# Four graph layers on one core: a finer last unit, another form of the state update, norms on ScalarE, row sums and bias additions on VectorE, and a start that streams one batch

## The chip, the cores and the metric

The kernel runs on one core of a Trainium2 chip. The time is the device time of one execution in microseconds (us). Its engines are TensorE (PE: matmuls, with PEld for their weight loads), VectorE (DVE), ScalarE (ACT), GpSimd (POOL) and SyncE (SP, whose queue starts most DMAs). On-chip memory is SBUF; matmuls write to the eight banks of PSUM, 128 rows of 512 fp32 each.

## The reference, cut to what matters

B = 8 batches of x with N = 1024 nodes and D = 128 features, and one adj of 1024 x 1024. Four layers follow each other, each as x = layernorm(x + layer(x)):

```python
# layer 0
adj @ (x @ W0) + b0
# layer 1
res = si[:, :, None] + sj[:, None, :] + adj * w_r + g_b    # si, sj = x @ w_i, x @ w_j
(res @ x) @ W1 + b1
# layer 2
x_h = elu(x @ Wi + bi)
e = sigmoid(a_tgt[:, :, None] + a_src[:, None, :] + be) * mask   # from x_h; mask from adj
recv = concat(e @ x_h, x_h * e.sum(-1))
concat(elu(recv @ Wn + bn), x_h) @ Wm + bm
# layer 3, five steps, in_matrix = out_matrix = adj
av = concat(adj @ h, adj @ h); u3 = h @ u3_w.T + u3_b
z = sigmoid(av @ w3_w.T + w3_b + u3)
r = sigmoid(av @ w4_w.T + w4_b + u3)
hv = tanh(av @ w5_w.T + w5_b + (r * h) @ u5_w.T + u5_b)
h = (1.0 - z) * h + z * hv
```

## The kernel before

**Precision.** Products with adj and those of layer 3 split each factor in a high part (rounded to fp32r by a ScalarE copy) and a low part (what is left, a DVE subtraction called `lo`, L1023), and add hi x hi, hi x lo and lo x hi: three matmuls in place of one. `adj_product` (L617 to L624) does it for one half of 512 columns: 8 tiles x 3 = 24 matmuls of 128x512. The other matmuls take plain fp32.

**Pieces and units.** Layers 0 to 2 of a batch are cut into named pieces: `x0` (load and split), `m0a m0b` (product with adj, by halves), `y0a y0b` (weights and sum with x), `v0` (statistics of the norm), `n0` (its power -0.5 and application), then `l1`, `d1` (split, row dots), `sums`, `rows`, `m1`, `y1`, `v1`, `n1` of layer 1, and `t2`, `pj`, `th`, `tg`, `as`, `s00` to `s17`, `e00` to `e17`, `rs`, `rv`, `y2`, `v2`, `n2` of layer 2. `s01` is a sigmoid of one tile (ScalarE, L907) and its product with the mask (DVE, L1168) in a ring of three slots; `e01` the matmul on it (L719); its row sums are added tile by tile by GpSimd (L591), and `rsa` (L725) broadcasts them. GpSimd also adds the bias rows b0 and bm to x (`add_bias`, L562) and takes each norm's power (L574, L602, L605).

Layer 3 runs in 40 units, one for a step of a batch; two batches alternate. Unit u makes `state_product` for its own batch and, between the pieces of that, the candidate and the update of the unit before. Its DVE update (L1195 to L1203) is

```python
v = v - hT        # L1198, after tanh
v = v * z         # L1200
hT = hT + v       # L1202
```

A table written by hand or by a planner (`TABLES`) gives for each engine the order of the pieces: a `first` list that runs before unit 0, and for each unit the numbered gaps (`@4`) in which pieces are put. Each engine follows its own list in order; semaphores join them. Batches 0 to 3 are mostly prepared ahead of unit 0 and in units 0 to 7; batches 4, 5 from unit 10, and 6, 7 from unit 20 on. After a batch's fifth step the next unit takes its statistics (`output_stats`) and, at its end, applies the norm on DVE (`output_apply`, L1046); SP stores it.

**Start.** SP loads x of batch 0, one tile of adj, x of batch 1, the other seven tiles, then weights and x of batches 2 and 3. ScalarE and DVE split each tile as it comes; TensorE multiplies batches 0 and 1 with each tile (L829 to L840), 12 matmuls a tile, after both batches have been split.

**End.** After unit 39 (batch 7, step 5) the candidate, the update, the turn back, the sum with x, eight statistics, the power, eight applications and one store of 512 KB follow one another.

## Time and profile before

| | us |
|---|---|
| median of 3 runs | 1278.41 (1275.87 to 1279.11) |
| the profiled execution | 1275.51 |
| its span in the trace | 1273.7 |
| TensorE busy | 1221.2 |
| VectorE busy | 924.8 |
| ScalarE busy | 587.7 |
| GpSimd busy | 267.5 |
| mean granted TensorE clock | 0.987 |

The span runs from the first instruction to the last one in the trace; the execution's own time is 1.8 us more. A busy time counts each moment once in which the engine worked on something. A granted clock of 1.00 is 2.4 GHz, 0.50 is 1.2 GHz.

### The profile page before, as it was taken

How to read it: one execution, taken by the hardware profiler on the slowest of the kernel's cores; microseconds unless marked ns; L12 is line 12 of the kernel's file. 1: busy time of each engine (PE TensorE's matmuls, PEld its weight loads, DVE VectorE, ACT ScalarE, POOL GpSimd, SP SyncE). 2: the span in 40 equal slices, each digit the busy share in tenths (PEclk: the TensorE clock that was granted, in tenths of full speed). 3: DMA queues.
4: the chain of work that ended last, by engine and by line, in shares of the span. 5: the costliest groups of instructions: out<-in, count | busy, mean ns of one | idle time of the engine just before them, and what ended most of it. 6: DMA issues, size and time to landing. Idle time of an engine off the chain costs nothing.

```text
span 1273.7 us, 15433 instructions
## 1 busy us (share of the span) xinstructions
PE 1221.2 (96%) x5488; PEld 937.0 (74%) x5488; DVE 924.8 (73%) x2154; ACT 587.7 (46%) x857; POOL 267.5 (21%) x174
## 2 busy tenths in 40 slices
PE   6988889999999999999999999999999999999994
PEld 5866457577777888877787688886787688888883
DVE  6999776867766586679587676688777768655656
ACT  4225653546654434355345553336446544444451
POOL 3115561511420010035013311024202500000001
PEclk9989999999999999999999999999999999999997
DMA  7212221200200011012002101102101200000001
GB/s 242 100 58 82 78 90 42 83 26 1 91 18 1 1 34 59 1 40 86 9 1 67 42 1 38 54 1 76 58 1 33 75 2 17 17 1 1 1 1 33
DMA packets 38459, 52.70 MB, mean 41 GB/s; under 512 B 2736, under 2 KB 19632, under 8 KB 38384
## 3 DMA queue, kind: packets, MB, share of 16 engines
q1 hardware_dynamic: 38240, 51.33, 12.2%
q8 instruction: 44, 0.72, 0.2%
q0 software_dynamic: 144, 0.40, 0.1%
q14 instruction: 31, 0.25, 0.1%
HBM read 43.32 MB, written 8.39 MB: 41 GB/s over the span
## 4 chain that ended last, share of the span: by engine, by line
PE 85%; DVE 9%; issue 2%; ACT 2%; POOL 1%; DMA 1%; POOLq 0%; SPq 0%; DVEq 0%; ACTq 0%
PE ps L622 44%; PE ps L719 7%; PE ps L627 6%; PE ps L629 6%; PE ps L628 6%; PE ps L633 4%; PE ps L640 3%; PE ps L837 2%; PE ps L732 1%; PE ps L725 1%; PE ps L733 1%; DVE x L1046 1%; DVE ring L1168 1%; PE ps L700 1%; PE ps L681 1%
## 5 line engine op out<-in xcount | busy, mean ns | idle before, releaser
L622 PE MATMUL ps<-adj_hi,xh 128*128 128x512 f32 x656 | 282.2, 430 | 3.6 <-DVE xl L1023 2.5
L622 PE MATMUL ps<-adj_hi,xl 128*128 128x512 f32 x656 | 257.2, 392 | 0.0
L622 PE MATMUL ps<-adj_lo,xh 128*128 128x512 f32 x656 | 256.4, 391 | 0.0
L622 PEld LDWEIGHTS ps<-adj_hi,xh 128*128 128x128 f32 x656 | 123.7, 189 | 41.8 <-issue 15.5
L622 PEld LDWEIGHTS ps<-adj_lo,xh 128*128 128x128 f32 x656 | 123.9, 189 | 32.4 <-issue 10.6
L591 POOL TENSOR_TENSOR fr<-fr,ring 128x512 f32<-128x512 f32 x84 | 125.0, 1488 | 106.0 <-DVE ring L1168 102.9
L622 PEld LDWEIGHTS ps<-adj_hi,xl 128*128 128x128 f32 x656 | 123.3, 188 | 27.1
L1168 DVE TENSOR_TENSOR ring<-ring,mk 128x512 f32<-128x512 f32 x128 | 102.3, 832 | 39.5 <-ACT ring L907 39.3
L1186 DVE TENSOR_TENSOR r<-r,hT 128x512 f32<-128x512 f32 x80 | 71.2, 907 | 77.8 <-ACT r L960 77.8
L863 ACT ACTIVATE mh<-ps 128x512 fp32r<-128x512 f32 x80 | 47.7, 596 | 167.3 <-PE ps L622 167.3
L719 PE MATMUL ps<-ring,fz 128*128 128x512 f32 x224 | 109.6, 600 | 4.2 <-DVE ring L1168 3.9
L1023 DVE TENSOR_TENSOR ml<-ps,mh 128x512 fp32r<-128x512 f32 x80 | 55.1, 688 | 76.9 <-ACT mh L863 76.6
L627 PE MATMUL ps<-mh,wh 128*128 128x512 f32 x240 | 104.5, 435 | 1.6 <-DVE ml L1023 1.5
L907 ACT ACTIVATE ring<-fh,asrcm 128x512 f32<-128x512 f32 x112 | 77.1, 718 | 48.2 <-PE ps L719 30.1
L629 PE MATMUL ps<-ml,wh 128*128 128x512 f32 x240 | 93.9, 391 | 0.0
L628 PE MATMUL ps<-mh,wl 128*128 128x512 f32 x240 | 93.7, 390 | 0.0
L863 ACT ACTIVATE xh<-ps 128x512 fp32r<-128x512 f32 x64 | 38.1, 595 | 117.3 <-PE ps L633 117.3
L627 PE MATMUL ps<-th,wh 128*128 128x512 f32 x160 | 73.7, 461 | 2.5 <-DVE tl L1023 2.5
L960 ACT ACTIVATE r<-ps,cols 128x512 f32<-128x512 f32 x80 | 54.5, 689 | 46.1 <-PE ps L629 45.6
L602 POOL TENSOR_TENSOR rso<-veo,mhalf 128x8 f32<-128x8 f32 x7 | 12.6, 1802 | 292.2 <-DVE veo L1041 292.2
L952 ACT ACTIVATE z<-ps,cols 128x512 f32<-128x512 f32 x80 | 54.1, 687 | 36.9 <-PE ps L629 36.6
L719 PEld LDWEIGHTS ps<-ring,fz 128*128 128x128 f32 x224 | 40.9, 191 | 35.2 <-issue 21.0
...
## 6 DMA issues: line engine op xcount, KB each, us to landing
mk<-mask_scratch SPq DMA_DIRECT2D x128, 256.0 KB, 2.9
...
```

Source lines behind the costliest of these rows:

```text
L591: tell(pool.tensor_tensor(f["r"][:, cut(h)], before, ring[:, k % RING, :], ALU.add), "rs_" + name[1:], b)
L622: mm = pe.matmul(dst, a[:, t, :], b[:, t, cut(h)], start=(t == 0 and i == 0), stop=(t == T - 1 and i == 2))
L627: pe.matmul(dst, wh[:, k, :], hi, start=first, stop=False, skip_group_check=True)
L628: pe.matmul(dst, wl[:, k, :], hi, start=False, stop=False, skip_group_check=True)
L629: return pe.matmul(dst, wh[:, k, :], lo, start=False, stop=last, skip_group_check=True)
L719: tell(pe.matmul(ps[:, BANKS_B[b][h], :], f["z"][:, tile(t)], ring[:, place[b, h, t] % RING, :], start=(t == 0), stop=(t == T - 1)), "ag" ...
L863: return act.activation(dst, src, ACT.Copy)
L907: tell(act.activation(ring[:, k % RING, :], f["h"][:, cut(h)], ACT.Sigmoid, bias=f["asrc"][:, t:t + 1]), "sg" + name[1:], b)
L960: act.activation(r[:, cut(h)], ps[:, GB + h, :], ACT.Sigmoid, bias=rb).then_inc(r_done, 1)
L1023: return dve.tensor_tensor(dst, src, hi.bitcast(F32), ALU.subtract)
L1168: tell(dve.tensor_tensor(ring[:, k % RING, :], ring[:, k % RING, :], mk[:, k % RING, :], ALU.mult), "ma" + name[1:], b)
L1186: dve.tensor_tensor(r[:, cut(h)], r[:, cut(h)], hT[s][:, cut(h)], ALU.mult).then_inc(rh_done, 1)
```

## The change

1. **Last unit by halves.** Unit 39 gets an order of its own (`ending`) on TensorE, ScalarE and DVE: gates, reset and candidate of half 0 (512 columns) run inside and behind the product of half 1, and the last batch's output is normed and stored as two halves. The second half's norm is applied on DVE.
2. **Update** as v = v z; hT = v - (z - 1) hT. The product (z - 1) hT (`keep`) is made before tanh, after the low part of the reset.
3. **Norms applied on ScalarE**, as Identity(scale x + bias) with scale rs and bias nb = -mean rs, a new 128x8 product on GpSimd behind the power. The mean's factor is -0.5 in place of 0.5.
4. **Row sums and bias additions on DVE**: each tile's addition stands right behind its mask product; new pieces `c0` and `c2` add the bias rows.
5. **Batch 0 alone streams**: batch 1's x is loaded after all of adj, and its m0 runs as ordinary pieces.
6. All four tables have a new order.

The orders, cut to the first lists of TensorE, ScalarE and DVE and a few units:

```diff
     "PE": """
-first m0a:0 m0b:0 m0a:1 m0b:1 y0a:0 y0b:0 y0a:1 y0b:1 m0a:2 m0b:2 y0a:2 y0b:2 m1a:0 m1b:0 sums:0 m1a:1
-first rows:0 y1a:0 m1b:1 y1b:0 sums:1 rows:1 y1a:1 t2a:0 t2b:0 pja:0 pjb:0 y1b:1 tha:0 thb:0 tga:0 tgb:0
-first m1a:2 m1b:2 e00:0 e01:0 e02:0 sums:2 e03:0 e04:0 e05:0 t2a:1 t2b:1 rows:2 y1a:2 e06:0 e07:0 pja:1
...
-first pja:2 pjb:2 e10:1
+first m0a:0 m0b:0 y0a:0 y0b:0 m0a:1 m0b:1 y0a:1 y0b:1 m0a:2 m0b:2 m1a:0 m1b:0 sums:0 m1a:1 rows:0 y1a:0
+first m1b:1 y1b:0 sums:1 y0a:2 y0b:2 rows:1 y1a:1 y1b:1 t2a:0 t2b:0 pja:0 pjb:0 tha:0 thb:0 tga:0 tgb:0
+first m1a:2 t2a:1 m1b:2 e00:0 e01:0 e02:0 e03:0 t2b:1 e04:0 sums:2 pja:1 e05:0 e06:0 e07:0 rows:2 rsa:0
+first pjb:1 y1a:2 y1b:2 e10:0 rva:0 e11:0 tha:1 e12:0 e13:0 thb:1 y2a:0 tga:1 tgb:1 e14:0 e15:0 e16:0 e17:0
+first rsb:0 rvb:0 e00:1 e01:1 e02:1 m0a:3 y2b:0 e03:1 e04:1 e05:1 m0b:3 e06:1 e07:1 y0a:3 y0b:3 t2a:2 t2b:2
+first e10:1
...
     "ACT": """
+first x0:0 x0:1 x0:2 m0a:0 m0b:0 weights:0 m0a:1 m0b:1 n0:0 m0a:2 n0:1 m0b:2 m1a:0 m1b:0 m1a:1 m1b:1 n1:0
+first t2a:0 t2b:0 pja:0 pjb:0 n0:2 tha:0 thb:0 tga:0 tgb:0 n1:1 s00:0 s01:0 s02:0 t2a:1 m1a:2 m1b:2 s03:0
...
     "DVE": """
-first x0:0 x0:1 x0:2 weights:0 mask:0 mask:1 mask:2 y0a:0 mask:3 y0b:0 y0a:1 v0:0 y0b:1 mask:4 n0:0 v0:1
-first l1:0 d1:0 n0:1 mask:5 l1:1 d1:1 sums:0 mask:6 y0a:2 mask:7 rows:0 y0b:2 y1a:0 v0:2 y1b:0 v1:0 sums:1
-first n0:2 n1:0 rows:1 pja:0 pjb:0 y1a:1 y1b:1 l1:2 as:0 v1:1 s00:0 s01:0 s02:0 d1:2 n1:1 s03:0 s04:0 s05:0
+first x0:0 c0:0 x0:1 x0:2 y0a:0 c0:1 weights:0 y0b:0 mask:0 v0:0 mask:1 c0:2 y0a:1 y0b:1 mask:2 v0:1 l1:0
+first d1:0 mask:3 l1:1 d1:1 mask:4 mask:5 mask:6 sums:0 mask:7 rows:0 y1a:0 y1b:0 v1:0 sums:1 y0a:2 y0b:2
+first rows:1 v0:2 c2:0 y1a:1 pja:0 pjb:0 y1b:1 v1:1 l1:2 as:0 d1:2 s00:0 s01:0 s02:0 s03:0 s04:0 s05:0 s06:0
+first c2:1 s07:0 sums:2 pja:1 rows:2 s10:0 rsa:0 s11:0 pjb:1 s12:0 s13:0 y1a:2 rva:0 y1b:2 v1:2 s14:0 s15:0
...
     "POOL": """
+first n0:0 n0:1 n1:0 n0:2 n1:1 n1:2 n2:0 n0:3 n1:3 n2:1 n2:2 n2:3
```

The code, cut to its core (the first `ending` is that of TensorE, the second that of DVE; `norm_apply` is ScalarE's):

```diff
             load(0)
             for t in range(T):
                 sp.dma_start(stage[t], adjT[tile(t), :]).then_inc(s_adj[t], 16)
-                if t == 0:
-                    load(1)
+            load(1)
...
+            def ending(now, prev):
+                s, p, i = now
+                state_product(s, 0, p, i, prev, {})
+                for h in range(2):
+                    candidate(*prev, halves=(h,))
+                for h in range(2):
+                    from_state(s, h, p, i, prev)
+                state_product(s, 1, p, i, prev, {1: lambda: (update_gate(s, 0, p, i), turn_state(prev[0], 0, *prev[1:])),
+                                                 2: lambda: turn_state(prev[0], 1, *prev[1:]),
+                                                 4: lambda: reset_gate(s, 0, p, i),
+                                                 6: lambda: candidate_start(s, 0, p, i, prev)})
+                candidate(*now, halves=(0,))
+                update_gate(s, 1, p, i)
+                candidate_start(s, 1, p, i, prev)
+                reset_gate(s, 1, p, i)
+                turn_state(s, 0, p, i)
+                candidate(*now, halves=(1,))
+                turn_state(s, 1, p, i)
...
+            def norm_apply(src, small_, tiles):
+                _, _, _, rs, nb = small_
+                for t in tiles:
+                    ins = act.activation(src[:, t, :], src[:, t, :], ACT.Identity, bias=nb[:, t:t + 1],
+                                         scale=rs[:, t:t + 1])
+                return ins
...
-            def update(s, p, i, fill=lambda: None):
-                for h in range(2):
+            def keep(s, p, i, halves=(0, 1)):
+                for h in halves:
+                    dve.wait_ge(rh_done, nth(p, i, s, h))
+                    dve.scalar_tensor_tensor(out=hT[s][:, cut(h)], in0=z[:, cut(h)], scalar=1.0, in1=hT[s][:, cut(h)],
+                                             op0=ALU.subtract, op1=ALU.mult).then_inc(kept, 1)
+
+            def update(s, p, i, fill=lambda: None, halves=(0, 1)):
+                for h in halves:
                     dve.wait_ge(v_done, nth(p, i, s, h))
-                    dve.tensor_tensor(v[:, cut(h)], v[:, cut(h)], hT[s][:, cut(h)], ALU.subtract).then_inc(d_sub, 1)
-                    dve.wait_ge(d_sub, nth(p, i, s, h))
                     dve.tensor_tensor(v[:, cut(h)], v[:, cut(h)], z[:, cut(h)], ALU.mult).then_inc(d_mul, 1)
+                    dve.wait_ge(kept, nth(p, i, s, h))
                     dve.wait_ge(d_mul, nth(p, i, s, h))
-                    dve.tensor_tensor(hT[s][:, cut(h)], hT[s][:, cut(h)], v[:, cut(h)], ALU.add).then_inc(h_new, 1)
+                    dve.tensor_tensor(hT[s][:, cut(h)], v[:, cut(h)], hT[s][:, cut(h)], ALU.subtract).then_inc(h_new, 1)
                     fill()
...
+            def ending(now, prev):
+                s, p, i = now
+                m_split(s, 0, p, i)
+                update(*prev)
+                state_lo(prev[0], 0, *prev[1:])
+                state_lo(prev[0], 1, *prev[1:])
+                reset(s, p, i, halves=(0,))
+                output_stats(B - 2)
+                reset_lo(s, p, i, halves=(0,))
+                keep(s, p, i, halves=(0,))
+                output_moments(B - 2)
+                m_split(s, 1, p, i)
+                update(*now, halves=(0,))
+                reset(s, p, i, halves=(1,))
+                state_lo(s, 0, p, i)
+                reset_lo(s, p, i, halves=(1,))
+                keep(s, p, i, halves=(1,))
+                output_stats(B - 1)
+                update(*now, halves=(1,))
+                output_moments(B - 1)
+                state_lo(s, 1, p, i)
+                output_stats(B)
+                output_moments(B)
+                output_apply(B)
```

## Rows read from the trace of the kernel before

**Rows 1.** The page, section 1: busy us (share of the span) xinstructions.
```profile
PE 1221.2 (96%) x5488; PEld 937.0 (74%) x5488; DVE 924.8 (73%) x2154; ACT 587.7 (46%) x857; POOL 267.5 (21%) x174
```

**Rows 2.** Busy time by stretch: length, each engine, granted clock, DMA share, GB/s.
```profile
0.00:96.00 96.00, 79.84 (x385) 65.79 (x386) 81.61 (x241) 27.08 (x33) 21.89 (x22) 0.95 0.38 133
96.00:178.00 82.00, 70.35 (x281) 44.08 (x280) 66.42 (x191) 45.57 (x61) 43.56 (x27) 0.98 0.25 81
178.00:240.00 62.00, 58.49 (x247) 40.22 (x246) 51.31 (x169) 26.50 (x37) 22.80 (x14) 0.95 0.16 51
240.00:1234.00 994.00, 990.55 (x4482) 769.72 (x4481) 697.84 (x1483) 477.96 (x711) 175.98 (x110) 1.00 0.09 29
1234.00:1274.00 40.00, 21.97 (x100) 17.17 (x98) 27.59 (x73) 10.61 (x17) 3.27 (x2) 0.83 0.09 26
```

**Rows 3.** Groups by form: 1100 to 1230 us, 96 to 240 (two), whole run (two).
```profile
L1186 DVE TENSOR_TENSOR r<-r,hT 128x512 f32<-128x512 f32 x14 | 9.6, 692 | 24.3 <-ACT r L960 24.3
...
L1168 DVE TENSOR_TENSOR ring<-ring,mk 128x512 f32<-128x512 f32 x39 | 29.6, 796 | 1.8 <-ACT ring L907 1.8
...
L1168 DVE TENSOR_TENSOR ring<-ring,mk x39: 672/682/2068, 100.0 to 239.4; 128x512 f32<-128x512 f32 x39
...
L1186 DVE TENSOR_TENSOR r<-r,hT 128x512 f32<-128x512 f32 x80 | 71.2, 907 | 77.8 <-ACT r L960 77.8
...
L591 POOL TENSOR_TENSOR fr<-fr,ring 128x512 f32<-128x512 f32 x84 | 125.0, 1488 | 106.0 <-DVE ring L1168 102.9
```

**Rows 4.** Timeline of the start (start, length, engine); first row: the chain.
```profile
11.11 23.80 PE ps L837 x96
...
7.54 1.23 DVE L1023 TENSOR_TENSOR adj_lo<-fh,adj_hi 128x1024 fp32r<-128x1024 f32 x1
...
11.11 0.77 PE L837 MATMUL ps<-adj_hi,fxh 128*128 128x512 f32 x1 [11.11 <-DVE xl L1023]
...
14.25 3.42 DVE L1023 TENSOR_TENSOR adj_lo<-fk,adj_hi 128x1024 fp32r<-128x1024 f32 x1
...
18.68 1.07 ACT L863 ACTIVATE adj_hi<-v 128x1024 fp32r<-128x1024 f32 x1 [0.28 <-DMA v<-in_adjT]
...
24.87 2.62 DVE L1060 TENSOR_TENSOR mk<-mk 128x128 f32<-128x128 f32 x3 [0.40 <-DMA mk<-in_u]
```

**Rows 5.** Timeline around m1a of batch 2, rsa of batch 0, and unit 0.
```profile
94.50 1.21 DVE L1023 TENSOR_TENSOR tl<-x,th 128x1024 fp32r<-128x1024 f32 x1
...
95.77 0.50 PE L622 MATMUL ps<-adj_hi,th 128*128 128x512 f32 x1
...
119.89 2.25 POOL L591 TENSOR_TENSOR fr<-fr,ring 128x512 f32<-128x512 f32 x1
...
122.19 1.13 PE L725 MATMUL ps<-fr,ones 128*128 128x512 f32 x2 [1.38 <-POOL fr L591]
...
177.65 0.50 PE L622 MATMUL ps<-adj_hi,xh 128*128 128x512 f32 x1 [2.16 <-DVE xl L1023]
```

**Rows 6.** Groups of ScalarE by form, whole run.
```profile
L952 ACT ACTIVATE z<-ps,cols 128x512 f32<-128x512 f32 x80 | 54.1, 687 | 36.9 <-PE ps L629 36.6
...
L863 ACT ACTIVATE mh<-ps 128x512 fp32r<-128x512 f32 x80 | 47.7, 596 | 167.3 <-PE ps L622 167.3
L863 ACT ACTIVATE th<-r 128x512 fp32r<-128x512 f32 x80 | 47.2, 624 | 2.9 <-DVE r L1186 2.5
L863 ACT ACTIVATE th<-hT 128x1024 fp32r<-128x1024 f32 x40 | 42.1, 1051 | 0.0
...
L863 ACT ACT_TABLE_LOAD x1 | 1.3, 1283 | 0.7 <-PEq L1311 0.7
```

**Rows 7.** Timeline of the tail.
```profile
1259.69 0.63 PE L633 MATMUL ps<-ident,hT 128*128 128x128 f32 x4 [3.22 <-DVE hT L1202]
...
1263.59 1.64 DVE L1028 BATCH_NORM_STATS2 sto<-x 128x6 f32<-128x128 f32 x8
...
1267.84 2.14 DVE L1046 TENSOR_SCALAR x<-x,mvo,rso 128x128 f32<-128x128 f32 x8 [1.75 <-POOL rso L605]
```

More of the change, by code:

```diff
@@ L46 @@
+unit3 @2 t2b:3 @10 pja:3 @12 pjb:3 @16 tha:3 @17 thb:3 tga:3 @22 tgb:3
+unit4 @1 e00:3 @9 e01:3 @11 e02:3 @15 e03:3 @16 e04:3 e05:3 @17 e06:3 @18 e07:3 @20 rsa:3 @21 e10:3 @22 e11:3 @23 e12:3 @24 e13:3 rva:3 e14:3 @27 e15:3
+unit5 @11 e16:3 e17:3 y2a:3 @14 rsb:3 @16 rvb:3 @22 y2b:3
+unit6
+unit7
 unit8
 unit9
[L48 to L51 removed]
```

490 lines of the change are left out of this document (255 added, 235 removed).

## Prediction

> **What bounds the kernel now.** I read the page first: its engine line [rows 1] shows TensorE busy for 1221.2 of 1273.7 us, VectorE (DVE) for 924.8. Then the table by stretch [rows 2], with its granted clock. From 240 to 1234 us TensorE is busy for 990.55 of 994 us at full clock: nothing that shortens another engine's work can show there. TensorE's idle time is 16.16 us before 96 us, 11.65 us from 96 to 178, 3.51 us from 178 to 240 and 18.03 us after 1234: 49.4 us in all, and in those stretches the clock is 0.95, 0.98, 0.95 and 0.83, so some matmuls run at 1.2 instead of 2.4 GHz. The change does not alter what TensorE computes, so it can win only there: in the head (to 240) and in the tail.
>
> In the head DVE is busy for 81.61 of 96 us and 66.42 of 82. The views by line and form say with what, and that GpSimd (POOL) makes it slower: r times h takes 692 ns where GpSimd is silent and 907 ns over the whole run; the mask product 796 ns from 96 to 240 although its median is 682 and its longest 2068 [rows 3]. So the question is what the new division of work does to DVE, and to the chains through it, before 240 us.
>
> **The start.** The first matmul is at 11.11 us [rows 4]. It waits for the low part of batch 1, though the first tile of adj is split at 7.54 + 1.23 = 8.77. With batch 0 alone it starts at about 8.8: 2.3 us won. Batch 0 brings 6 matmuls a tile; 96 matmuls take 23.80 us in the chain, the first nine of them at about 0.43 us and the rest at 0.227. Six at full speed take 1.4 us, and tiles arrive about every 1.3 us. GpSimd's first two bias additions, beside which one split took 3.42 instead of 1.23 us, are gone, and batch 1's 512 KB leave the queue between the tiles. The last tile, copied at 18.68 now, should be copied by 17.4 to 18.5 and split by 19.8; TensorE ends the stream at 21.2. Then y0 of batch 0 waits for ScalarE (the x copies of batches 1 and 2, then mc0a): 1.3 us idle. m0 of batch 2 starts at 36.9, against 38.48 now. The gain shrinks from 2.3 to 1.5 us.
>
> A first common mark is m1a of batch 2, because both orders have the same TensorE pieces ahead of it; it starts at 95.77 now, behind the low part of that batch, which DVE ends at 94.50 + 1.21 = 95.7 [rows 5]. Against that list DVE's new one has, ahead of the same point, four bias additions more (a 1024-column operation each, 1.22), the statistics v1 of batch 1 (1.64 + 0.9 = 2.55), four norm applications less (2.1 each), and it loses what GpSimd costs three sums of weights (2.62 us for three, where 128 columns take some 0.3 each: 1.8) [rows 4]: 4.9 + 2.5 - 8.4 - 1.8 = -2.8, which gives 92.9; ScalarE's norm ahead of the split, 1 us longer, makes it 93.9. TensorE's idle time there stays much as it is (5.05 us between 60 and 96; my layout of the new order has 4.3 ahead of the turn of x_h, 2.3 ahead of m1a:2, 1.7 in smaller pieces), and a us of slow clock goes with it: 94.8, so **-1 us**.
>
> **96 us to unit 0, now at 177.65** [rows 5]. TensorE takes 81.9 us for 66.8 us of work (pja and pjb of batch 2, 0.86 each, move behind unit 0's start: 65.1 afterwards). What was added to DVE: 31 row-sum additions at 0.69 (21.4 us) and three bias additions at 1.22 (3.7). What was taken off: six norm applications, which together take 17.6 us there. What GpSimd's contention costs there, from the forms against their quiet values (39 mask products at +0.114 are 4.4 us [rows 3]; the norm instructions, row dots, bias sums and clamps of that stretch make up the rest): about 18 us, of which 5 sit in the norm applications and 3 stay with GpSimd's remaining powers at 1.7. So 25.1 - 17.6 - 10 = -2.5 us: DVE's load is about the same, a little less.
>
> What changes more is the chains. Row sums took 1.49 us each on GpSimd [rows 3], and bias additions stand between them: the last one of batch 0's first half runs from 119.89 to 122.14, and the matmul on it waits till 122.19 [rows 5], though its mask product was done at 116.5. On DVE the addition stands 0.7 us behind the mask product. ScalarE also waits for GpSimd's sums to free the three ring slots. Against that, ScalarE's m1b copy now stands ahead of s03, which leaves DVE idle for some 4.5 us after s02. Laying both lists out on those durations, TensorE idles for 7.2 us (0.4 ahead of rows:2, 1.4 of e10:0, 1.1 of y2a:0, 0.4 of e14, 1.5 of rsb:0, 2.2 of rvb:0, 0.2 of m0a:3) and unit 0 starts at 166.2 + 1.7 (for the moved pieces) = 167.9, 9.7 us ahead. I take 1 us off this for the start's share (counted above), 2 for two ScalarE norms on the chain at +1 us each (below) and 2 for small waits and a half-speed stretch or two: **-5 us**, bounds 0 and -9.
>
> **Norms on ScalarE.** No row shows an application with two per-partition operands. DVE's eight instructions take 2.14 us in all [rows 7]. On ScalarE a copy of 128x512 from SBUF takes 624 ns and 128x1024 1051, so 0.83 ns a column and 0.2 us fixed; a per-partition bias makes 596 into 687, so +0.09 [rows 6]. With bias and scale: 0.107 + 0.2 + 0.18 = 0.48 us, less about 0.1 of overlap (the ring activations): 0.38, eight of them 3.1 us. Bounds 2.0 (plain copies of 128 columns) and 3.9. GpSimd adds a 128x8 product, 0.2 to 0.3 us. So each norm's chain grows by 1.0 + 0.3. Outside the head TensorE hides it: ScalarE is busy for 478 of 994 us, and the next split of m is 2.8 us away. All copies together cost one table load [rows 6]; I assume that Identity needs none either.
>
> The Trainium skill's page "ScalarE: Activation LUTs", section "Rules for kernel authors", speaks against this part: additions and products belong on VectorE. The rows bear it out for one instruction. That is rival 2.
>
> **Update as z v - (z - 1) h.** Three DVE instructions a half remain; one moves ahead of tanh. From tanh to the new state it is 2 x 0.72 instead of 3 x 0.72. In the full units TensorE never waits for it: 0. A scalar_tensor_tensor takes 750 ns where a product takes 690, 80 x 0.06 = 5 us of DVE, hidden by the 30% that DVE is idle there. Without that cover it would cost at most those 5.
>
> **The full units**: 0, bounds -2 (3.45 us are idle) and +4 (a 3.1 us output norm against a ScalarE gap of 2.8 in seven units, if the surplus always shows with its restart).
>
> **The tail** [rows 7]. Now: TensorE waits 3.22 us for the update alone; the statistics stand at 1263.59, power 1.64, application 2.14 to 1269.98, then a store of 3.7. Afterwards, with the same last-unit start of 1233.79: both products and their inserts end at 1250.1 (all passes at 0.68, turns 0.4). In the half order, r h of half 0 is at 1248.4, but batch 6's statistics (1.64) come ahead of its split, and its moments (0.9) ahead of m_split of half 1, so ml is ready only at 1253.0. Then reset gate 1255.4, r and its split 1258.5, tanh 1260.05, product and difference 1261.55, turn, moments of half 0, sum with x 1263.2, statistics and moments of four tiles 1.75, power 1.64, application of four tiles 1.07: 1267.7. **-2.3 us**, bounds 0 and -4.
>
> **Sum**: 1275.5 (that execution's time; span 1273.7 and 1.8 around it) - 1 - 5 + 0 - 2.3 = 1267.2. The median of the runs is 2.9 above that execution: 1270.1, so **1270**.
>
> **Rivals.**
> 1. The gain is the walk's in full: -1.5 - 9.7 - 2.3 and 1.5 more from a shorter unit 0: 15 us, 1263. For it: DVE's contention vanishes. Against: the walk has no small waits. The Trainium skill, "SBUF — State Buffer", section "Who interferes with whom", has a VectorE instruction with two SBUF inputs blocked whole while GpSimd reads; [rows 3] agree (2068 against 682 ns).
> 2. ScalarE's applications lengthen the chains: nine norms lie in the head, each +1.3 us. If all are on TensorE's path that is 11.7 us, of which I counted 2; the head's 6 us are gone and only the tail stays: 1276. For it: the idle gaps now sit at norms (81.3 to 85.5 us). Against: DVE does other work meanwhile.
> 3. Slower: DVE becomes longer. Per batch +14 x 0.69 + 2 x 1.22 - 3 x 2.1 = +5.8 us; four batches in the head make 23 us. It decides where contention gives back under 4 us a batch and the DVE list, not a chain, sets the pace: +10 of those 23 in view less the tail's 2 gives 1286. Against: the measured contention, 18 us for under three batches.
> 4. The new order works, but the tail alone shows, since ScalarE blocks on m1b and the ring waits come back: -2 to -3, 1276.
>
> **Chances.** Forecast 1270: 0.52; rival 1: 0.20; rivals 2 and 4 together: 0.18; rival 3: 0.10. A measurement of this kernel tells about 0.3% (3.8 us) from nothing. Faster: the forecast, rival 1 and a little of 2: 0.77; same 0.15; slower 0.08. The range leaves out rival 3 and half of rival 1's far side: 1259 to 1277; the forecast's own is 1266 to 1274.
>
> **What would show it.** Right: first matmul near 8.8; unit 0's first matmul (the first wait for the low part of batch 0's state) near 171; mask products near 690 ns; ScalarE applications near 0.38 us apart; still one table load for copies; the full units at over 99.5%; the last application ending some 2 us nearer to unit 39's start. Wrong: DVE over 90% busy from 96 to 178, TensorE waiting for norms, or idle time in the full units.

## The result, and the profile after

The changed kernel takes 1264.18 us (median of 4 runs, 1263.86 to 1265.89) against 1277.28 for the kernel before beside it; the ratio is 0.9902, 95% interval 0.9885 to 0.9918. It is faster by 13 us; 1270 was forecast. The profiled execution took 1264.36 us, its span is 1262.6, so 1.8 us lie around the span as before. Ratios are taken over executions of the fast state; one execution of a later kernel (e11) took 2549.81 us, in the slow state, and is not in its ratio.

The engine line of the page, which answers to [rows 1]:

```profile
PE 1217.9 (96%) x5488; PEld 935.6 (74%) x5488; DVE 870.5 (69%) x2037; ACT 683.0 (54%) x1109; POOL 73.2 (6%) x79
```

TensorE's work is the same 5488 matmuls; VectorE lost 54 us, GpSimd 194, ScalarE gained 95. The table by stretch, with the columns of [rows 2] and bounds moved to the new marks:

```profile
0.00:96.00 96.00, 77.45 (x383) 63.57 (x384) 76.53 (x242) 39.00 (x65) 14.89 (x24) 0.98 0.38 133
96.00:170.00 74.00, 68.17 (x275) 42.73 (x274) 57.57 (x159) 51.08 (x81) 5.41 (x4) 0.99 0.27 86
170.00:240.00 70.00, 65.72 (x271) 44.86 (x272) 54.56 (x165) 40.13 (x69) 6.61 (x6) 0.95 0.19 61
240.00:1222.00 982.00, 979.59 (x4446) 763.85 (x4445) 656.25 (x1404) 535.24 (x865) 42.16 (x40) 1.00 0.09 29
1222.00:1263.00 41.00, 26.92 (x119) 20.63 (x117) 25.59 (x70) 17.55 (x32) 4.12 (x5) 0.86 0.09 26
```

Before 96 us TensorE idles for 18.55 us, 2.4 more than before; from 96 us to unit 0 it idles for 5.8 us, where [rows 2] give 11.65. The middle is 99.8% busy.

TensorE's busy time fell too, by 3.3 us for the same 5488 matmuls, because less of it lies at the lower of the two clock levels (granted clock 0.50): before unit 39, the kernel before is there from 79.8 to 90.0, 124.1 to 127.5, 178.8 to 182.2 and 236.8 to 240.2 us, the changed kernel from 91.2 to 98.1 and 231.2 to 238.1. In these stretches it is busy for 17.2 against 10.7 us, and half the difference is 3.3 us. So of the 11.1 us between the two spans 7.8 are idle time of TensorE (52.5 and 44.7 us), and the other 3.3 are what the clock is worth.

The timeline of TensorE: the first matmul, y0 of batch 0, and unit 0's first matmul, against [rows 4, 5]:

```profile
8.68 0.77 PE L855 MATMUL ps<-adj_hi,fxh 128*128 128x512 f32 x1 [8.68 <-DVE adj_lo L1078]
...
22.81 2.02 PE L631 MATMUL ps<-wf,fm 128*128 128x128 f32 x16 [1.06 <-ACT fm L878]
...
170.43 0.80 PE L613 MATMUL ps<-adj_hi,xh 128*128 128x512 f32 x1
```

The first matmul is 2.4 us earlier and unit 0 7.2 us earlier. Between them lies the mark, m1a of batch 2. This is the chain of work (start, length, what) that leads to it:

```profile
83.33 1.57 DVE stAp L1086 x8
...
85.83 2.59 POOL rsAp L572
...
88.49 0.21 POOL nbAp L574
...
88.73 3.19 ACT x L883 x8
91.95 1.06 ACT th L878
93.00 0.49 ACT fz L878
93.50 0.14 issue
93.63 3.75 PE ps L702 x4
97.39 2.65 PE ps L613 x10
```

TensorE pipelines its matmuls, so the first one of the mark is drawn from 96.40 on, beside the end of those before it; the second is the safer mark. The first row is the low part of batch 2, which the mark needs:

```profile
93.04 1.23 DVE L1078 TENSOR_TENSOR tl<-x,th 128x1024 fp32r<-128x1024 f32 x1
...
97.61 0.61 PE L613 MATMUL ps<-adj_lo,th 128*128 128x512 f32 x1
```

In the kernel before it starts at 96.11, 0.34 us behind the row in [rows 5], so the mark is now **1.5 us later**. TensorE waits 3.10 us at 93.63 for `fz`, ScalarE's copy of `tha` of batch 0. ScalarE could not make it, for the norm of batch 2 (its eight applications and the rounding) stands ahead of it in its list. That wait is not the mark waiting for batch 2: its low part is done at 94.27, 3.3 us ahead. It is another batch's copy queued behind a norm. The norm in its turn starts when VectorE's statistics and GpSimd's power of 2.59 us are done; VectorE works without a break from 74.54 to 85.77 on this chain.

The four matmuls that waited then take 3.75 us, at a granted clock of 0.50, where the kernel before has, at 1.00:

```profile
94.00 2.04 PE L711 MATMUL ps<-fk,we2b 128*128 128x512 f32 x4
```

The groups by form, whole run, which answer to [rows 3] (VectorE) and [rows 6] (ScalarE):

```profile
L1227 DVE TENSOR_TENSOR ring<-ring,mk 128x512 f32<-128x512 f32 x128 | 87.2, 686 | 35.1 <-ACT ring L933 35.1
L1234 DVE TENSOR_TENSOR fr<-fr,ring 128x512 f32<-128x512 f32 x84 | 58.2, 692 | 9.1 <-DVE ring L1227 0.5
...
L1252 DVE TENSOR_TENSOR r<-r,hT 128x512 f32<-128x512 f32 x80 | 54.4, 691 | 88.9 <-ACT r L990 88.9
...
L1264 DVE SCALAR_TENSOR_TENSOR hT<-z,hT 128x512 f32<-128x512 f32 x80 | 51.6, 685 | 0.0
```

```profile
L883 ACT ACTIVATE x<-x,nbAm,rsAm 128x128 f32<-128x128 f32 x80 | 31.9, 484 | 7.0 <-POOL nbAm L574 7.0
...
L878 ACT ACT_TABLE_LOAD x1 | 1.3, 1283 | 0.7 <-PEq L1410 0.7
```

With GpSimd quiet, r times h takes 691 ns in place of 907. An application is 484 ns by itself, and eight of them 3.18 us, since they overlap. Copies and applications together still have one table load, and all of ScalarE has 48, before and after.

The tail, timeline, against [rows 7]:

```profile
1243.09 0.50 PE L618 MATMUL ps<-th,wh 128*128 128x512 f32 x1 [0.25 <-DVE tl L1078]
...
1250.63 0.50 PE L618 MATMUL ps<-th,wh 128*128 128x512 f32 x1 [2.46 <-DVE tl L1078]
...
1253.98 1.09 PE L624 MATMUL ps<-ident,hT 128*128 128x128 f32 x4 [2.39 <-DVE hT L1273]
...
1257.60 1.01 POOL L581 TENSOR_TENSOR rso<-veo,mhalf 128x4 f32<-128x4 f32 x1 [1.70 <-DVE veo L1104]
1258.65 1.11 DVE L1365 TENSOR_SCALAR x<-x,mvo,rso 128x128 f32<-128x128 f32 x4 [1.12 <-POOL rso L581]
```

Four columns of the power take 1.01 us where eight took 1.64, and the span ends 2.84 us after the last application, not 3.72: the last store is half as large.

By marks, the two spans differ as follows (us):

| stretch | before | changed | difference | forecast |
|---|---|---|---|---|
| start to the second matmul of m1a, batch 2 | 96.11 | 97.61 | +1.5 | -1 |
| from there to unit 0's first matmul | 81.54 | 72.82 | -8.7 | -5 |
| unit 0 to unit 39 | 1056.14 | 1055.66 | -0.5 | 0 |
| unit 39 to the end of the span | 39.91 | 36.51 | -3.4 | -2.3 |
| sum | 1273.7 | 1262.6 | -11.1 | -8.3 |

The profiled execution of before (1275.51) was 1.8 us faster than the median beside the changed kernel's (1277.28), and the changed kernel's was 0.2 us slower than its own: that is the other 2 us of the 13.

The second row is not all gain. `pja` and `pjb` of batch 2, 1.7 us of TensorE's work, have moved behind unit 0's start. Of the 8.7 us, 5.8 are idle time (11.65 to 5.82 us), 1.7 are these two pieces, and the rest, 1.2 us, has the size of the stretch of half clock at 124.1. Units 0 to 39 have taken the pieces in and are shorter by 0.5 us all the same; their idle time explains 0.3 of these 2.2 us (6.96 to 6.69 us), the rest is open.

### The profile page after: what moved, and what is told of

Same layout as the page of the kernel before. It is cut to its first block, busy times and chain, and to the rows that moved or that the text cites. A ratio compares the mean times of both kernels' runs of the same rounds, so it can differ in the third digit from the quotient of the medians.

```text
span 1262.6 us, 15547 instructions
## 1 busy us (share of the span) xinstructions
PE 1217.9 (96%) x5488; PEld 935.6 (74%) x5488; DVE 870.5 (69%) x2037; ACT 683.0 (54%) x1109; POOL 73.2 (6%) x79
## 4 chain that ended last, share of the span: by engine, by line
PE 85%; DVE 7%; ACT 3%; issue 2%; POOL 1%; SPq 1%; DMA 1%; POOLq 0%; DVEq 0%; ACTq 0%
PE ps L613 45%; PE ps L618 7%; PE ps L620 7%; PE ps L619 7%; PE ps L710 6%; PE ps L631 4%; PE ps L624 4%; ACT x L883 2%; DVE ring L1227 1%; PE ps L702 1%; PE ps L716 1%; PE ps L723 1%; PE ps L724 1%; PE ps L672 1%; PE ps L691 1%
## 5 line engine op out<-in xcount | busy, mean ns | idle before, releaser
L613 PE MATMUL ps<-adj_hi,xh 128*128 128x512 f32 x672 | 293.1, 436 | 2.0 <-DVE ml L1078 1.6
L613 PE MATMUL ps<-adj_hi,xl 128*128 128x512 f32 x672 | 263.4, 392 | 0.0
L613 PE MATMUL ps<-adj_lo,xh 128*128 128x512 f32 x672 | 262.7, 391 | 0.0
L613 PEld LDWEIGHTS ps<-adj_hi,xh 128*128 128x128 f32 x672 | 126.7, 189 | 41.8 <-issue 18.6
L613 PEld LDWEIGHTS ps<-adj_lo,xh 128*128 128x128 f32 x672 | 126.9, 189 | 35.9 <-issue 13.9
L613 PEld LDWEIGHTS ps<-adj_hi,xl 128*128 128x128 f32 x672 | 126.4, 188 | 27.8
L1252 DVE TENSOR_TENSOR r<-r,hT 128x512 f32<-128x512 f32 x80 | 54.4, 691 | 88.9 <-ACT r L990 88.9
L1227 DVE TENSOR_TENSOR ring<-ring,mk 128x512 f32<-128x512 f32 x128 | 87.2, 686 | 35.1 <-ACT ring L933 35.1
L620 PE MATMUL ps<-ml,wh 128*128 128x512 f32 x240 | 93.9, 391 | 0.0
L1078 DVE TENSOR_TENSOR xl<-ps,xh 128x512 fp32r<-128x512 f32 x64 | 43.9, 686 | 42.8 <-ACT xh L878 42.8
L710 PEld LDWEIGHTS ps<-ring,fz 128*128 128x128 f32 x224 | 40.6, 191 | 35.8 <-issue 15.9
L1234 DVE TENSOR_TENSOR fr<-fr,ring 128x512 f32<-128x512 f32 x84 | 58.2, 692 | 9.1 <-DVE ring L1227 0.5
```

Of the source, the lines that this page charges most:

```text
L613: mm = pe.matmul(dst, a[:, t, :], b[:, t, cut(h)], start=(t == 0 and i == 0), stop=(t == T - 1 and i == 2))
L620: return pe.matmul(dst, wh[:, k, :], lo, start=False, stop=last, skip_group_check=True)
L710: tell(pe.matmul(ps[:, BANKS_B[b][h], :], f["z"][:, tile(t)], ring[:, place[b, h, t] % RING, :], start=(t == 0), stop=(t == T - 1)), "ag" ...
L1078: return dve.tensor_tensor(dst, src, hi.bitcast(F32), ALU.subtract)
L1227: tell(dve.tensor_tensor(ring[:, k % RING, :], ring[:, k % RING, :], mk[:, k % RING, :], ALU.mult), "ma" + name[1:], b)
L1234: tell(dve.tensor_tensor(f["r"][:, cut(h)], first_sum, ring[:, k % RING, :], ALU.add), "rs_" + name[1:], b)
```

## The experiments

Which part makes the gain of the head? My theory (A): the row sums off GpSimd. Rivals: relief of VectorE by the norms (B), the order of the pieces alone (C). Seven kernels (e1 to e7) undo one part of the changed kernel or load it with more, e8 undoes four parts together; two do one part alone on the kernel before; one moves norms again; one tries an improvement. The table has their results. "Shift" is how much later than in the changed kernel ScalarE's first copy of a unit's first half product (mh) starts in the profiled executions, at four units; "tail" is from that copy of unit 39 to the end of the span.

| kernel | median | ratio to before, 95% | shift unit 0 | 5 | 20 | 39 | tail |
|---|---|---|---|---|---|---|---|
| changed | 1264.18 | 0.9902 (0.9885-0.9918) | 0 | 0 | 0 | 0 | 30.9 |
| before | 1277.28 | 1 | 6.5 | -0.4 | 9.1 | 7.7 | 34.3 |
| e1 tail whole | 1266.46 | 0.9922 (0.9909-0.9934) | 0.2 | -0.9 | -0.9 | -0.9 | 33.7 |
| e2 sums on GpSimd | 1276.38 | 0.9996 (0.9987-1.0005) | 4.7 | 6.6 | 9.5 | 11.4 | 31.5 |
| e3 norms on VectorE | 1316.92 | 1.0316 (1.0299-1.0332) | 6.1 | 13.1 | 32.7 | 50.7 | 31.5 |
| e4 old update | 1270.62 | 0.9946 (0.9932-0.9960) | 0.9 | 3.5 | 5.6 | 6.8 | 32.2 |
| e5 junk on GpSimd | 1328.00 | 1.0398 (1.0383-1.0412) | 15.9 | 30.5 | 42.3 | 62.7 | 30.9 |
| e6 biases on GpSimd | 1267.98 | 0.9927 (0.9915-0.9939) | 0.1 | -0.3 | 0.3 | 2.4 | 30.8 |
| e7 two batches stream | 1273.47 | 0.9969 (0.9958-0.9980) | 8.0 | 6.9 | 6.9 | 6.8 | 31.5 |
| e8 old operations, new order | 1331.21 | 1.0421 (1.0404-1.0437) | 18.6 | 25.9 | 46.8 | 63.4 | 32.7 |
| e9 as e3, norms later | 1306.44 | 1.0217 (1.0196-1.0239) | 6.4 | 12.9 | 24.6 | 41.2 | 31.5 |
| e10 before, sums on VectorE | 1288.22 | 1.0081 (1.0066-1.0097) | 9.0 | 6.7 | 18.9 | 19.9 | 34.2 |
| e11 before, norms on ScalarE | 1345.76 | 1.0528 (1.0507-1.0549) | 21.6 | 29.6 | 59.4 | 77.5 | 34.2 |
| e12 two edits | 1263.78 | 0.9894 (0.9874-0.9913) | -0.6 | -0.6 | -0.2 | -0.2 | 30.5 |

In the middle, before and changed put different pieces into the same units, so before's shifts at units 5 and 20 say little. The shifts come from one execution each, and executions of one kernel differ: e4's (1269.20 to 1272.58) by 3.4 us, and the profiled one is its slowest. Differences in time below are those of the ratios.

**e1, the last unit whole.** TensorE's, ScalarE's and VectorE's `ending` is replaced by the general unit and what follows it:

```diff
-            ending(*units[-1])
+            end = units[-1][0]
+            update(*end)
+            for h in range(2):
+                state_lo(end[0], h, *end[1:])
+            output_stats(B - 1)
+            output_moments(B - 1)
+            output_apply(B - 1)
```

> The changed kernel with part 1 undone: the last unit in the order of all others, batch 7's output normed as a whole, its application on ScalarE, and one store of 512 KB. The same is computed. The changed kernel's trace has 36.5 us from unit 39's first matmul to the end of the span, the kernel before 39.9. Theory A (the halves are worth what the two traces differ by): the tail gets 3 to 4 us longer, 1264.2 becomes about 1267.5, all of it behind unit 39's start; unit 39 starts within 0.5 us of the changed kernel's 1226.1, and after the last application there is about 3.7 us again in place of 2.84. Rival (the tail got shorter by the ScalarE application and the other update, not by the halves): the tail gets longer by less than 1.5 us, time about 1265.

Measured: the tail is 2.8 us longer, unit 39 0.9 us earlier, the time 0.2% (2.6 us) longer, with intervals that overlap. The end of its timeline has before's durations back:

```profile
1257.00 1.64 POOL L581 TENSOR_TENSOR rso<-veo,mhalf 128x8 f32<-128x8 f32 x1 [11.52 <-DVE veo L1106]
1258.67 2.14 DVE L1367 TENSOR_SCALAR x<-x,mvo,rso 128x128 f32<-128x128 f32 x8 [1.75 <-POOL rso L581]
```

Theory A, a little under its 3 us; the rival (below 1.5) fell. At its end the halves save 0.8 us of statistics (1.65 to 0.87), 0.6 of power, 1.0 of application and 0.9 of store, 3.3 in all; the order of the halves gives some 0.5 of it back ahead of the last statistics. The expectation says that e1's last application is on ScalarE. It is on VectorE (L1367), as the last one is in the kernel before and in the changed kernel, so ScalarE's application cannot be what shortens the end. The update has a part in it: with the old one the tail is 1.3 us longer (e4), so the two parts share the 3.4 us and do not add up to it.

**e2, row sums back on GpSimd**, in the order of VectorE's list:

```diff
-  {"ACT": ..., "DVE": ("ma" + piece[1:],) + (("rs_" + piece[1:],) if a != "0" else ())}
+  {"ACT": ..., "DVE": ("ma" + piece[1:],), "POOL": ("rs_" + piece[1:],) if a != "0" else ()}
...
+ tell(pool.tensor_tensor(f["r"][:, cut(h)], first_sum, ring[:, k % RING, :], ALU.add), "rs_" + name[1:], b)
```

> The changed kernel with the row sums of the attention back on GpSimd (84 additions of 128x512, in the order that VectorE's list gives them); bias additions stay on VectorE, norm applications on ScalarE. The same is computed. Unit 0's first matmul is at 170.4 in the changed kernel. Theory A (the gain of the head is from taking the sums off GpSimd): VectorE's reset products go from 691 to 800 or more ns each, the last sum of batch 0 ends 1 to 2 us behind its mask product, the matmul that broadcasts it waits, and unit 0 starts 2 to 5 us later, time about 1267. Rival B (the gain is from the relief of VectorE by the norms) or C (from the new order alone): unit 0 starts within 1 us of 170.4, and the time is 1264 to 1265 or less, since VectorE has 84 x 0.69 = 58 us less of its own.

Measured: unit 0 4.7 us later, as A had it, but then it goes on, to 11.4 us at unit 39: the whole gain is gone. Groups by form:

```profile
L1256 DVE TENSOR_TENSOR ring<-ring,mk 128x512 f32<-128x512 f32 x128 | 106.3, 858 | 55.4 <-ACT ring L962 54.8 <-DMA mk<-mask_scratch 0.5
L1274 DVE TENSOR_TENSOR r<-r,hT 128x512 f32<-128x512 f32 x80 | 60.1, 762 | 95.0 <-ACT r L1019 95.0
...
L602 POOL TENSOR_TENSOR fr<-fr,ring 128x512 f32<-128x512 f32 x84 | 120.6, 1436 | 120.4 <-DVE ring L1256 117.6
```

It is the mask product, on the chain of the attention, that pays (686 to 858 ns); r times h goes to 762, not to 800. TensorE's waits for the ring rise from 4.9 us in 5 to 10.1 in 12. ScalarE now waits for GpSimd's sums before it can fill a slot of the ring, 24.8 us in 17 waits, so e2 has both the contention and the longer chain, and does not part them.

**e3 and e9, all norms applied on VectorE**: one piece behind the statistics in e3, one more in e9.

```diff
-        return {"POOL": ("rs" + a, "nb" + a), "ACT": ("xn" + a,)}
+        return {"POOL": ("rs" + a,), "DVE": ("xn" + a,)}
...
+ dve.tensor_scalar(src[:, t, :], src[:, t, :], mv[:, t, 0:1], rs[:, t:t + 1], ALU.add, ALU.mult)
```

> The changed kernel with every norm applied on VectorE as (x - mean) rs, one piece behind its statistics, without the small product on GpSimd; the rest is as changed. The same is computed. Each norm then costs VectorE 8 x 0.25 to 0.27 = 2.1 us and ScalarE 3.2 us less. Theory A (ScalarE's applications cost a little at the start: the norm of batch 2 stands ahead of the roundings that m1a of batch 2 and the first tanh matmuls wait for): the start gets shorter, the mark of batch 2's m1a comes before 96.5 in place of 97.4, and unit 0 within 1 us of 170.4: the time is the same, 1262 to 1265. Rival B (relief of VectorE by the norms is what made the stretch before unit 0 shorter): unit 0 starts at least 3 us later, time 1267 or more.

> As the run with all norms on VectorE, but each application one piece (or gap) later, so that GpSimd's power is there when VectorE comes to it: in that run VectorE stood still for 19.8 us before the applications, and the time was 1316.9. The same is computed. If that standing still made the loss, the wait goes below 8 us and the time falls to 1285 or less. If it is the 64 us of work that VectorE gets (8 x 0.34 us for each of 31 norms) in an order that has no room for it, the time stays above 1300.

Theory A fell: e3 is 53 us slower than the changed kernel (1.0316 against 0.9902), with 6.1 us of it at unit 0. The 3.1 us for `fz` are gone, but the mark is 3.1 us later still, at 100.74: TensorE waits for VectorE, which stands at norms, in two other places:

```profile
85.45 2.04 PE L652 MATMUL ps<-wf,z 128*128 128x128 f32 x8 [5.06 <-DVE kba L1222]
...
95.11 0.63 PE L645 MATMUL ps<-ident,fk 128*128 128x128 f32 x4 [3.88 <-DVE fk L1234]
```

B has the right sign and half the place: most of the loss lies in the full units. How much is work and how much standing still? VectorE's waits for GpSimd's power, in e3 and then in e9:

```profile
DVE x L1102 <- POOL rsAm L598: 13.1, 10, 1.8
DVE x L1102 <- POOL rsBm L598: 6.7, 5, 1.8
...
```

```profile
DVE x L1110 <- POOL rsAm L606: 9.8, 9, 1.8
DVE x L1110 <- POOL rsBm L606: 5.9, 4, 1.8
...
```

With the smaller ones they are 27.6 us in e3 (the expectation of e9 counted only the two rows shown, 19.8; its 8 x 0.34 us for each norm would also be 84 us, and 64 is 31 times the 2.07 us that eight take) and 17.5 in e9: 10.1 us less, and the time is 10.5 us less. The time stays above 1300, as the second reading said, but the waits did not fall below 8 us, as the first needs, so e9 does not settle it; what is left, 40 us above the changed kernel with 17.5 us of waits, leaves room for both causes. What TensorE waits for in e3's units is VectorE: from 188 us to the end of unit 39, 36.9 us for `ml`, the ring and `tl` in its three largest groups, where the changed kernel has 5.3 us.

**e4, the old update**, (v - h) z + h, with nothing ahead of tanh:

```diff
-  v = v * z;  hT = v - hT        # hT holds (z - 1) hT, made by keep
+  v = v - hT;  v = v * z;  hT = hT + v
```

> The changed kernel with the update as before: v - h, times z, added to h, all behind tanh, and no product ahead of it. The same is computed. Full units are over 99.5% busy on TensorE in both, so behind tanh one more operation of 0.69 us for each half falls where TensorE has other matmuls. Theory A (the form of the update is hidden in full units): units 0 to 38 take the same time within 1 us, and only the last unit gets longer, by one 128x512 operation for each half that the end waits for (0.7 to 1.4 us): time 1264.5 to 1266. Rival D (a unit loses part of the 0.7 us each time): 40 x 0.2 us or more, time 1272 or more.

Measured: 0.44% (5.6 us) slower than the changed kernel; units 0 to 38 lose 5.9 us, the tail 1.3 (in the profiled execution, e4's slowest, 8.1 us in all). Neither of the two: it is not 0.2 us in every unit, for from unit 30 on nothing is lost. 2.6 us go in units 0 to 5 and 3.3 more up to unit 32, where the gaps are filled with pieces. From 180 to 420 us TensorE is busy for 235.64 us in the changed kernel and 233.37 in this one (first row that of the changed kernel, tables by stretch):

```profile
180.00:420.00 240.00, 235.64 (x1018) 173.84 (x1017) 167.27 (x358) 135.45 (x217) 9.39 (x10) 0.99 0.11 36
```

```profile
180.00:420.00 240.00, 233.37 (x1009) 172.07 (x1008) 166.20 (x355) 135.08 (x216) 10.29 (x10) 0.99 0.11 36
```

From unit 0 to unit 39 TensorE's idle time is 10.7 us against 6.7. So the earlier state is not free of worth: TensorE hides the step in a bare unit, and does not where pieces stand between. (4.0 of the 5.9 us are idle time; where the other 1.9 go is open.)

**e5, contention alone**: GpSimd adds a tile of its own to itself at each mask product that has a row sum (112), and nobody reads it or waits for it.

```diff
+                elif name[0] == "s" and name[1:].isdigit():
+                    seen(pool, "ma" + name[1:], b)
...
+                    pool.tensor_tensor(ghost[:, :], ghost[:, :], ghost[:, :], ALU.add).then_inc(s_ghost, 1)
```

> The changed kernel plus junk work: with each mask product whose row sum is taken (84 of them), GpSimd adds two 128x512 tiles of its own that nothing reads and that nobody waits for. VectorE keeps the row sums; the outputs are the same. It shows contention alone, without the longer chain. Theory A1 (part of the gain is that VectorE's and ScalarE's operations are not slowed any more by GpSimd's additions): VectorE's mask products and reset products go from 686 and 691 to 750 or more ns where a junk addition runs beside them, and unit 0 starts 1 to 4 us later than 170.4; the time is 1265 to 1268. Rival A2 (the chain, sum behind mask product on a slow engine, is all of it): unit 0 starts within 0.7 us, the time is the same.

Measured: 63 us slower than the changed kernel. Groups by form:

```profile
L1264 DVE TENSOR_TENSOR fr<-fr,ring 128x512 f32<-128x512 f32 x84 | 124.7, 1484 | 9.1 <-DVE ring L1257 0.5
L1257 DVE TENSOR_TENSOR ring<-ring,mk 128x512 f32<-128x512 f32 x128 | 89.2, 702 | 23.1 <-ACT ring L963 23.1
...
L1108 DVE TENSOR_TENSOR ml<-ps,mh 128x512 fp32r<-128x512 f32 x80 | 55.0, 687 | 65.5 <-ACT mh L908 65.5
...
L604 POOL TENSOR_TENSOR ghost<-ghost 128x512 f32<-128x512 f32 x112 | 121.4, 1084 | 402.4 <-DVE ring L1257 400.9
```

A1's sign, at far over its price, and not where I put it: the mask product stays at 702; the sum right behind it, which starts with GpSimd's addition, takes 1484 ns in place of 692. Only 6 of the 128 mask products run beside a junk addition (by over 0.15 us), and those take 1106 ns on average, the others 682. TensorE's waits for the ring rise from 4.9 us to 28.8 in 31. Contention by itself, with no chain through GpSimd, is enough to lose the head's gain. (There are 112 such additions, one for every sum; the expectation counted one group of 84. The norms' powers stand behind the junk in GpSimd's list, but none is late for it: the 33 powers start 2.7 us in all behind VectorE's results, 0.08 us each, as in the changed kernel.) It is not a price for the contention of the kernel before: here VectorE keeps the sums, and it is mostly they that meet GpSimd; there it is the mask products and r times h.

The subtraction that reads PSUM (`ml<-ps`) keeps its 687, but it runs beside a junk addition only once. The kernel before shows more: 14 of its 80 run beside a row sum or bias addition of GpSimd's and take 685 ns on average, the others 689; of the mask products 61 do, at 992 against 685, and of the products r times h 16, at 1776 against 690. The Trainium skill's page "SBUF — State Buffer", section "Who interferes with whom", says that a VectorE instruction with two SBUF inputs and a GpSimd instruction that reads SBUF lock each other out; the row of the sum agrees, and so do these counts for the instructions with two SBUF inputs.

**e6, bias additions on GpSimd:**

```diff
-        return {"DVE": ("xb" + a,)}
+        return {"POOL": ("xb" + a,)}
```

> The changed kernel with the bias additions of layers 0 and 2 (16 of 128x1024, 1.2 us each on VectorE) back on GpSimd. The same is computed. Theory A (they are a small part): unit 0 starts within 1 us of 170.4 and units 0 to 38 stay as they are, time 1263.5 to 1265. Rival (the bias additions are what the head's gain hangs on, since GpSimd's take some 3 us each and slow VectorE beside them): unit 0 over 2 us later, time 1266.5 or more.

Measured: unit 0 unmoved, 2.1 us lost between units 20 and 39, the time 0.25% (3.2 us) longer with intervals that overlap. A as to the head; the middle was not foreseen. 16 bias additions are a fifth of the moved work and a small part.

**e7, both batches stream:**

```diff
                 sp.dma_start(stage[t], adjT[tile(t), :]).then_inc(s_adj[t], 16)
+                if t == 0:
+                    load(1)
-            load(1)
...
+ for b in range(2):   # 12 matmuls a tile in TensorE's stream
```

> The changed kernel with part 5 undone: batch 1's x is loaded behind the first tile of adj, and both batches are multiplied with each tile as it arrives, 12 matmuls a tile; the other orders are those of the changed kernel, but that batch 1's m0 stands in the stream. The same is computed. In the changed kernel the first matmul is at 8.68, m1a of batch 2 at 97.39. Theory A (streaming one batch starts TensorE earlier, and the waits that follow take most of it back, by waiting for roundings on ScalarE): the first matmul comes at about 11, the mark at 97 to 99, and unit 0 within 1.5 us of 170.4; time 1263.5 to 1266. Rival (the early start is kept in full): mark and unit 0 both 2 to 3 us later, time 1266.5 or more.

The rival's sign held, at over twice its price: the mark is 6.7 us later (second matmul at 104.34), unit 0 8.0 us, the time 0.67% (8.6 us) longer. The first matmul (11.04) is only 2.4 us later; what counts is y0 of batch 0, on TensorE's timeline:

```profile
34.80 1.95 PE L632 MATMUL ps<-wf,fm 128*128 128x128 f32 x16
...
40.72 3.75 PE L632 MATMUL ps<-wf,z 128*128 128x128 f32 x16 [3.97 <-ACT z L881]
```

It starts 12 us later than the 22.81 of the changed kernel, so VectorE's and ScalarE's chain of batch 0 starts 12 us later.

**e8, old operations in the new order** (e2, e3, e4 and e6 together, with the moved pieces placed by the same rules as there):

> The changed kernel's orders, start, and last unit, with the operations of before: row sums and bias additions on GpSimd (in the order of VectorE's list), norms applied on VectorE, the update as v - h, times z, plus h. The same is computed. Theory C (the order of the pieces makes the gain of the head): unit 0 starts within 1.5 us of 170.4 and the time is within 2 us of 1264.2. Theory A (the moved operations make it, the order was made to suit them): unit 0 starts 4 to 8 us later, 175 to 178, and the time is 1268 to 1273.

Both theories fell: 66 us slower than the changed kernel and 54 slower than before, which has the same operations in another order (and no last unit by halves). The new order, with the old operations put into it by rule, is a large loss.

**e10, the kernel before with sums and biases on VectorE alone**, and **e11, before with the norms of layers 0 to 2 on ScalarE alone**: the moved pieces are put into the old lists by rule.

```diff
+        if name in ("y0a", "pja"):
+            out.append(("c0" if name == "y0a" else "c2", b))     # e10, VectorE's list
...
+            if name == "t2a":
+                out.append(("n1", b))                           # e11, ScalarE's list
```

> The kernel before with one part alone: row sums and bias additions on VectorE (each sum right behind its mask product, each bias addition ahead of the first piece that needs it), GpSimd's list only the norms' powers; orders, norms, update, start and last unit as before. The same is computed. Its own marks: batch 2's m1a at 95.8, unit 0 at 177.7. If moving these operations is worth something by itself (no contention, 0.69 us in place of 1.45 for each sum), the time is 2 to 8 us below the kernel before (1276.4): 1268 to 1274, and unit 0 starts 3 us earlier or more. If an order fits only the durations that it was made for, VectorE's added 78 us come late in some of the units' gaps, and the time is equal or above 1276, with units 12 to 18 and 22 to 28 longer.

> The kernel before with one other part alone: the norms of layers 0 to 2 (24 of them) are applied on ScalarE with the small product on GpSimd behind the power; those of layer 3's outputs stay on VectorE; n1 stands ahead of the first copy that needs it in ScalarE's list, n2 a gap or two behind its statistics. The same is computed. If the application on ScalarE is a cost on the chain of a batch (3.2 us in place of 2.1, and GpSimd's product 0.4) and no gain elsewhere, the start gets up to 4 us longer and the time is 1277 to 1282. If relief of VectorE is worth something in the old order too, as the run with the norms back on VectorE suggests for the new one, the time is below 1274.

e10 is 0.81% (10 us) slower than before: the second reading in sign, though not in place, for of the 12.2 us that it is behind before at unit 39, 7.1 are lost by unit 5. Its engine line, and TensorE's wait for the ring, which was 3.9 us in 4:

```profile
PE 1224.9 (95%) x5488; PEld 935.3 (73%) x5488; DVE 940.3 (73%) x2282; ACT 588.8 (46%) x857; POOL 60.1 (5%) x46
```

```profile
PE ps L708 <- DVE ring L1157: 7.0, 10, 2.2
```

VectorE got 112 sums at 0.69 and 16 bias additions at 1.22, 97 us, and is busy for only 15.5 us more than before [rows 1]. The other 81 us (97 less 15.5) came back from contention, and the time rose all the same. e11 is 5.3% slower, more than either side said. That the old lists put nothing between the statistics and the readers of the norm is my reading of it; TensorE's waits for the application, which is in no other run:

```profile
PE ps L661 <- ACT x L914: 37.4, 8, 8.6
```

A rule that puts pieces into a list is a poor planner: e3, e8, e9, e10 and e11 bound what a part does without an order that suits it, and not its best.

**e12, two edits to the changed kernel:**

```diff
-first ... pja:0 pjb:0 n0:2 tha:0 thb:0
+first ... pja:0 pjb:0 tha:0 n0:2 thb:0
...
-                output_stats(B - 2)          # ahead of reset_lo of half 0
...
                 update(*now, halves=(0,))
+                output_stats(B - 2)
+                output_moments(B - 2)
```

> The changed kernel with two edits: ScalarE applies the norm n0 of batch 2 behind the first copy of the attention's transposed product (tha) of batch 0, in place of ahead of it, and the last unit takes the statistics of batch 6 behind the update of its first half. The same is computed. In the changed kernel TensorE waits 3.1 us for that copy at 93.6, and 2.4 us for the first half's new state at 1254. Theory: the first wait goes, and batch 2's m1a starts 1 to 3 us before 97.4, but unit 0 comes only 0 to 2 us earlier, since batch 2's chain is put off by the same copy; the tail gets 0.7 to 1.4 us shorter: time 1260.5 to 1263.5. Rival: the chain of batch 2 is what binds until unit 0, so that unit 0 comes 0 to 1 us later, and the tail's statistics only move the wait to VectorE: time 1264 to 1265.

Measured: 0.9894 against 0.9902, no difference that can be told; the time, 1263.78, lies between the theory's range and the rival's. On ScalarE's timeline the first copy now stands ahead of the norm, the second behind it, and TensorE waits for that one:

```profile
89.12 0.60 ACT L878 ACTIVATE fz<-ps 128x512 f32<-128x512 f32 x1 [2.14 <-PE ps L624]
89.61 3.17 ACT L883 ACTIVATE x<-x,nbAp,rsAp 128x128 f32<-128x128 f32 x8
...
93.78 0.58 ACT L878 ACTIVATE fz<-ps 128x512 f32<-128x512 f32 x1
```

```profile
94.50 2.05 PE L702 MATMUL ps<-fk,we2b 128*128 128x512 f32 x2 [3.44 <-ACT fz L878]
```

The mark's second matmul comes 0.8 us earlier (96.77) and unit 0 0.6: less than the theory said at the mark, since the wait has only moved; the tail gains 0.4 us and not 0.7, since half 1's reset product now waits for the statistics.

## Why the prediction was right, and where it was not

The mechanism was right: time can be won only in head and tail, it was won there, and the result, 1264, lies in the range. It lies below the forecast's own 1266 to 1274 and nearer to rival 1's 1263 than to 1270. Of the 5.8 us between forecast and result 1.1 are the median of before, 1277.28 here and 1278.41 there. Rival 1's number came near, but not by its account: it has 1.5 + 9.7 = 11.2 us from the start to unit 0, where the 9.7 already held the start's share, and there are 7.2. The sum of the terms, -8.3 for -11.1, is off by 2.8 us and its terms by 7.8 together, for errors of both signs stand in it. By the steps:

- **First matmul** at 8.8: 8.68. **The start** of -1 was wrong, it is +1.5. The count of VectorE's work held: it had the low part of batch 2 split at 93.9, and it is done at 94.27. The step that failed is that the mark goes by that low part, and with it "TensorE's idle time there stays much as it is": TensorE was not there to take it. It stood at `fz` for 3.10 us until 93.63, and the four matmuls behind that wait, which come before the mark, took 3.75 us at half clock. My own layout of TensorE's idle time there had 8.3 us against 5.05, and I passed over it; TensorE now waits 3.1 us for `fz`, 2.7 for `fk` and 1.9 for `kba`, and 1.1 in smaller pieces, 8.8 in all. The norm on ScalarE I charged to its own batch's chain and not to the `fz` copies that stand behind it. Earlier, m0 of batch 2 starts at 37.40 against 38.24 (not 38.48, the end of the piece ahead of it): 0.8 us of the 1.5 that the walk had left.
- **96 us to unit 0** at -5 was too little: -8.7. Of this 1.7 us are the pieces moved behind unit 0's start, which the forecast had counted back in, so it is 7.0 by the forecast's own measure. TensorE idles there for 5.8 us; my layout had 7.2, and I added 4 for norms and small waits, which did not come in this stretch. The norm's cost came before the mark instead. Head and stretch together are at -5.5 by that measure, against -6 forecast and -9.7 by the layout: the place came out nearly right (171.6 forecast, 170.43 measured) because the two errors have opposite signs, and that is luck. Of the causes, e2 puts 4.7 us of unit 0's start on the row sums, e3 6.1 on the norms and e7 8.0 on the start, over 18 for a gain of 7.2, so none of these is a share of it.
- What I did not see in part 5: not the first matmul's 2.3 us, but the end of the stream 12 us earlier for batch 0 is what it is worth in this order (e7, 8 us at unit 0).
- **Norms on ScalarE**: 3.1 us for eight forecast, 3.18 measured; GpSimd's product 0.2 to 0.3 forecast, 0.23 to 0.46 measured as means of the groups and 0.20 to 1.22 singly; one table load, as assumed. That they are a cost only was wrong for this order: e3 and e9 lose 40 to 53 us without them. Rival 2 is refuted at its price, though its mechanism is there at the mark.
- **Update at 0**: as a difference between the two kernels the full units are at -0.5 us, as forecast, but with 1.7 us of moved work in them, so -2.2 by the forecast's measure, just beyond its bound of -2, and for 1.9 of that the traces give no reason. As a reason, "TensorE never waits for it" was wrong: e4 loses 5.9 us in units that have pieces. The instruction, with both inputs in SBUF, took 685 ns and not 750, which the trace of before has for the same operation with an input in PSUM.
- **Tail** -2.3: -3.4 in the traces, of which e1 shows 2.8 to go with the halves (and e4 1.3 with the update; they overlap). I used 1.64 us for a power on four columns (1.01) and 3.7 for the store (2.84); the last application ended 33.7 us after unit 39's start, where I had 33.9.
- Rival 3 (VectorE becomes longer) was far off: it is busy for 57.57 of 74 us before unit 0. Rival 4 fell by the -8.7.

What the prediction's sum hides is that its terms do not add. Undone one at a time in the changed kernel, the last unit costs 2.6 us, the row sums 12.0, the norms 53 (e9: 40), the update 5.6, the bias additions 3.2 and the start 8.6, over 70 together, where all of them gained 13; sums and biases alone in the old order cost 10, and the new order with the old operations 54. As far as these placements go, operations and order are a gain only together. Which share belongs to which is therefore not a question these runs can answer, and how much of e3's, e8's and e11's loss a better placing would take back stays open.
